# The first iteration's products in two passes, rounded parts before low parts, and VectorE's low parts in another order

## The chip, the cores and the metric

One core of one Trainium2 chip runs the whole kernel. Its engines are TensorE (PE: matmuls, with PEld for the weight loads), VectorE (DVE), ScalarE (ACT), GpSimd (POOL) and SyncE (SP, here only a queue that issues DMAs). Each works through its own queue in order; semaphores join them. The metric is the device time of one execution in microseconds, and the median of several is compared.

## The reference

The input x has 32 samples of 64 channels and 1024 points. Two levels follow each other, each `x = x + ffn(cond(x, style))`.

`cond` is four one-dimensional convolutions over the 64 channels whose weights depend on the sample (same, upsample with blur, same, downsample with blur). All four are linear with a bias, so the kernel folds the last three into one convolution per sample.

The ffn of level 0 is a routed adapter: `scores = x @ Wr.T` over 64 experts, the top 16 are kept and go through a softmax to gates, then `h = x @ A` (64 experts of rank 16, 1024 columns), `h` times the gate of its expert, and `out = 2 * (h @ B)`. The ffn of level 1 is a matmul with a 4-bit weight, dequantized with a scale and a zero for each column, and a bias.

## The kernel before, in words

**Precision.** TensorE multiplies in a rounded 32-bit format. So each operand is split into a rounded part `hi` (an ACTIVATE copy by ScalarE) and a low part `lo = whole - hi` (a subtraction by VectorE, helper `low`, L161), and each product is three matmuls: hi*hi, hi*lo, lo*hi. A and B are split so too, once, in eight chunks k of 128 rows: `act_a`/`dve_a` make `a_hi`, `a_lo`, `act_b`/`dve_b` make `b_hi`, `b_lo` (L952 and L161). `a_lo` lies over the loaded `a_raw`, `b_lo` over `b_raw`.

**Tiling.** Work goes by pairs of samples, 128 rows (two samples of 64 channels, or 128 tokens after the transposes). For level 0 a software pipeline over 16 pairs does in one pass the ffn of pair i and the convolutions of pair c = i+1. TensorE's order in one pass is: first layer of c, sample 0 (L175 to L177, 6 matmuls); transposes of the conv result of i (L739); first layer of c, sample 1; fold 3 of c (L593); hidden product, group 0 of i (`pe_hidden`, L766 to L768, 24 matmuls); fold 2 of c (L628); hidden groups 1 and 2; conv product of c, sample 0; transposes of the gated tile of i (L775); conv product of c, sample 1; adapter-out product of i, halves 0 and 1 (`pe_adapter_out`, L784 to L786, 24 matmuls each). Hidden group 0 (384 columns) holds the scores and the first 320 hidden columns, group 1 has 384, group 2 has 320. Each group has a PSUM bank of its own (`hidden_ps`).

**VectorE in one pass**: `dve_fold_start` (v_lo), `dve_turn` (low part of the transposed conv result, `xt`), `dve_layer1` (h_lo) for sample 0, `dve_fold3` (r_lo), `dve_layer1` for sample 1, `dve_route` (scores, top 16, exp, normalization), `dve_gate` 0, `dve_fold2` (e_lo and two copies), `dve_gate` 1 and 2, `dve_gated_turn` (low part of the turned gated tile, again `xt`), `split` (x_lo of the pair after next), `dve_first_residual`. ScalarE makes the rounded parts in the same order, with `act_exp` inside the routing.

**The first pass** (`first_pair(0, True)`) stands ahead of the loop over the others and has the splitting of A and B in it. Before it, ScalarE has made `a_hi` 0 to 6 and VectorE starts on `a_lo` 0 to 3. Inside it VectorE does `dve_a(4, 8)` right after `dve_turn`, `dve_b(0, 4)` after `dve_fold2`, and `dve_b(4, 8)` ahead of `dve_gated_turn`. ScalarE does `act_b(0, 3)` ahead of `act_exp` and `act_b(3, 8)` behind `act_fold2`. In hidden group 0 and adapter-out half 0 TensorE waits for the chunk's `a_lo` or `b_lo` ahead of each three matmuls. The queues' orders are written out by hand; no planner takes part.

Of the kernel before, what the change touches and what calls it, by code (L numbers as in the profile page):

```python
# [26 lines left out]
GROUPS = ((0, 384), (384, 768), (768, NE + KR))  # L27
ONES, QCOLS = 2, 342
KT = D // P
# [11 lines left out]
def program(nc, t):  # L41
    with ExitStack() as outer:
# [575 lines left out]
        def pe_fold2(pe, c, bufs, first=False):  # L618
            pe.wait_ge(S.fold3_ready, 2 * c + 2)
            if first:  # L620
                pe.wait_ge(S.lo["f2"], bufs.first_sample // B + 1)
            if not first or bufs.first_sample:
                pe.wait_ge(S.fold2_hi, 2 * c)
                pe.wait_ge(S.fold2_ready, c)
            for n, (tile, m, block) in enumerate(FOLD2):
                out = fold_ps[1][:, block * P:(block + 2) * P]
                for i, (w, r) in enumerate(((fold2_hi, bufs.r_hi), (fold2_hi, bufs.r_lo), (fold2_lo, bufs.r_hi))):
                    last = nc.tensor.matmul(out, windows(w)(tile), r[:, m:R_PAIRS:2, :, :], start=(n == 0 and i == 0),  # L628
                                            stop=(n == len(FOLD2) - 1 and i == 2), skip_group_check=True)
            last.then_inc(S.fold2_done, 1)  # L630
# [123 lines left out]

        hidden_ps = (prod_ps[0], prod_ps[1], turn_ps[1])

        def pe_hidden(pe, f, n, bufs, first=False):
            if n == 0:
                pe.wait_ge(S.xt_ready, 2 * f + 2)
                pe.wait_ge(S.x1_ready, 2 * f + 1)  # L760
            cols = slice(*GROUPS[n])
            out = hidden_ps[n][:, 0:cols.stop - cols.start]
            for k in range(KT):
                if first and n == 0:
                    pe.wait_ge(S.a_lo_ready, k + 1)
                nc.tensor.matmul(out, bufs.xt_hi[:, k, :], bufs.a_hi[:, k, cols], start=(k == 0), stop=False)  # L766
                nc.tensor.matmul(out, bufs.xt_hi[:, k, :], bufs.a_lo[:, k, cols], start=False, stop=False)  # L767
                last = nc.tensor.matmul(out, bufs.xt_lo[:, k, :], bufs.a_hi[:, k, cols], start=False, stop=(k == KT - 1))  # L768
            last.then_inc(S.hidden_done, 1)
# [8 lines left out]
        def pe_adapter_out(pe, f, bufs, n, first=False):  # L778
            pe.wait_ge(S.hgt_ready, 2 * f + 2)
            cols = slice(n * 512, (n + 1) * 512)  # L780
            for k in range(KT):
                if first and n == 0:
# [341 lines left out]
        def _(pe):  # L1124
# [16 lines left out]
            def first_step(i, first, conv=buf0):  # L1141
                c = i + 1
                second = conv is not buf0
                pe_layer1(pe, c, 0, conv, second)
                pe_turn(pe, i, buf0, False)
                pe_layer1(pe, c, 1, conv)
                pe_fold3(pe, c, conv, second)
                pe_hidden(pe, i, 0, buf0, first)
                pe_fold2(pe, c, conv, second)

            def first_products(i, first=False, conv=buf0):
                c = i + 1
# [3 lines left out]

            def first_pair(i, first):
                first_step(i, first)
                for n in (1, 2):
                    pe_hidden(pe, i, n, buf0)  # L1160
                first_products(i)
                for n in range(2):
                    pe_adapter_out(pe, i, buf0, n, first)

            first_pair(0, True)
            with pe.Fori(1, NPAIR - 2) as i:
# [94 lines left out]
        def _(act):  # L1261
# [44 lines left out]
            def first_step(i, first, conv=buf0):  # L1306
                c = i + 1
                second = conv is not buf0
                act_turn(act, i, buf0)
                if first:  # L1310
                    act_a(act, 7, KT)
                act_layer1(act, c, 0, conv)
                act_fold3(act, c, conv, second)
                act_layer1(act, c, 1, conv)
                if first:
                    act_b(act, 0, 3)
                act_exp(act, i, buf0)
                act_fold2(act, c, conv)
                if first:
                    act_b(act, 3, KT)  # L1320

            def first_pair(i, first=False):
                c = i + 1
# [107 lines left out]
        def _(v):  # L1431
# [34 lines left out]
            def first_step(i, first=False, conv=buf0):  # L1466

                c = i + 1
                dve_turn(v, i, buf0)
                if first:  # L1470
                    dve_a(v, 4, KT)
                dve_layer1(v, c, 0, conv)
                dve_fold3(v, c, conv)
                dve_layer1(v, c, 1, conv)

            def first_gates(i, first=False, conv=buf0):
                dve_route(v, i, buf0)
                dve_gate(v, i, 0, buf0)
                dve_fold2(v, i + 1, conv)
                if first:  # L1480
                    dve_b(v, 0, 4)

            def first_pair(i, first=False):
                c = i + 1
                dve_fold_start(v, c, buf0)
                first_step(i, first)
                first_gates(i, first)
                for n in (1, 2):
                    dve_gate(v, i, n, buf0)
                if first:  # L1490
                    dve_b(v, 4, KT)
                dve_gated_turn(v, i, buf0)
                split(c + 1, buf0)
                dve_first_residual(v, i, buf0)

# [166 lines left out]
```

## Time and profile before

| what | value |
|---|---|
| median of 3 runs | 946.69 us (945.65 to 946.77) |
| profiled execution: its own time | 946.65 us |
| its span (first to last instruction) | 945.0 us |
| TensorE busy (PE) | 920.9 us, 97% |
| weight loads (PEld) | 828.1 us, 88% |
| VectorE busy | 503.8 us, 53% |
| ScalarE busy | 410.0 us, 43% |
| GpSimd busy | 108.8 us, 12% |
| mean granted clock of TensorE | 0.987 |
| the chain that ended last: by engine | PE 89%, DVE 5%, ACT 2%, issue 2%, POOL 1% |

The busy shares are averages over the whole span. The matmul times of single rows include the drain of the pipeline, so that two rows overlap; the pitch of a stream is read from the starts. A wait is given for the instruction that stood still, with the one that released it.

### The profile page before, as it was taken

The page shows a single profiled execution, that of the slowest core. Times are in us where ns is not written, and L with a number is a line of the kernel's source. Part 1 is how long each engine was busy: PE and PEld are TensorE (multiplying, and loading weights), DVE is VectorE, ACT ScalarE, POOL GpSimd, SP SyncE. Part 2 cuts the span into 40 slices and gives each one's busy share as a digit, 9 for nine tenths or more (in the row PEclk, how much of TensorE's full clock was granted, in tenths as well). Part 3 has the DMA queues.
Part 4 walks back from the last instruction along what each step waited for, and adds up shares of the span by engine and source line. Part 5 has one row for each costly group of instructions (what it writes and reads, how often), then busy time and mean ns, then how long its engine had stood idle before and what let it go on. Part 6 is the DMA issues. An engine that isn't in the chain of part 4 may idle for free.

```text
span 945.0 us, 14656 instructions
## 1 busy us (share of the span) xinstructions
PE 920.9 (97%) x5020; PEld 828.1 (88%) x5020; DVE 503.8 (53%) x1079; ACT 410.0 (43%) x764; POOL 108.8 (12%) x137
## 2 busy tenths in 40 slices
PE   4889999999999999999999999999999999999998
PEld 4777998998998998998998998988999889998898
DVE  7795443443442442442452455578566656666555
ACT  2674333333333333432432433487455556555540
POOL 6100000000000000000000012130221112111121
PEclk9699999999999999999999999999999999999999
DMA  8701111011021011021021020225122222122111
GB/s 285 263 1 45 31 58 46 24 64 44 22 67 44 22 67 44 22 67 44 22 67 34 33 79 24 81 48 179 45 89 72 85 89 89 67 67 89 67 67 68
DMA packets 33004, 64.29 MB, mean 68 GB/s; under 512 B 11728, under 2 KB 13776, under 8 KB 32976
## 3 DMA queue, kind: packets, MB, share of 16 engines
q1 hardware_dynamic: 23904, 30.90, 11.0%
q0 software_dynamic: 9072, 33.03, 9.6%
q8 instruction: 16, 0.26, 0.1%
q14 instruction: 12, 0.10, 0.0%
HBM read 47.14 MB, written 16.78 MB: 68 GB/s over the span
## 4 chain that ended last, share of the span: by engine, by line
PE 89%; DVE 5%; ACT 2%; issue 2%; POOL 1%; SPq 0%; DMA 0%; ACTq 0%; DVEq 0%
PE conv_ps L175 9%; PE conv_ps L177 9%; PE conv_ps L176 9%; PE prod_ps L784 6%; PE prod_ps L786 6%; PE prod_ps L785 6%; PE fold_ps L628 5%; PE prod_ps L766 4%; PE prod_ps L768 4%; PE prod_ps L767 4%; PE prod_ps L860 4%; PE prod_ps L859 4%; PE fold_ps L593 3%; PE turn_ps L739 3%; PE turn_ps L768 2%; PE turn_ps L767 2%
## 5 line engine op out<-in xcount | busy, mean ns | idle before, releaser
L161 DVE TENSOR_TENSOR h_lo<-conv_ps,h_hi 64x512 fp32r<-64x512 f32 x128 | 88.3, 690 | 46.0 <-ACT h_hi L692 44.8
L175 PE MATMUL conv_ps<-h_hi,e_hi 128*128 128x512 f32 x256 | 104.3, 407 | 2.3 <-issue 1.8
L176 PE MATMUL conv_ps<-h_lo,e_hi 128*128 128x512 f32 x256 | 102.6, 401 | 0.0
L177 PE MATMUL conv_ps<-h_hi,e_lo 128*128 128x512 f32 x256 | 102.4, 400 | 0.0
L784 PE MATMUL prod_ps<-b_hi,xt 128*128 128x512 f32 x256 | 99.8, 390 | 1.5 <-DVE xt L161 1.5
L785 PE MATMUL prod_ps<-b_lo,xt 128*128 128x512 f32 x256 | 99.7, 389 | 0.0
L786 PE MATMUL prod_ps<-b_hi,xt 128*128 128x512 f32 x256 | 99.6, 389 | 0.0
L712 ACT ACTIVATE cond<-conv_ps,bias,demod_tab 128x510 f32<-128x510 f32 x64 | 49.8, 778 | 106.9 <-PE conv_ps L177 102.7
L766 PE MATMUL prod_ps<-a_hi,xt 128*128 128x384 f32 x256 | 86.9, 339 | 0.6 <-DVE a_lo L161 0.6
L768 PE MATMUL prod_ps<-a_hi,xt 128*128 128x384 f32 x256 | 86.5, 338 | 0.0
L767 PE MATMUL prod_ps<-a_lo,xt 128*128 128x384 f32 x256 | 86.4, 338 | 0.0
L859 PE MATMUL prod_ps<-quant,xt_hi 128*128 128x342 f32 x256 | 80.6, 319 | 0.0
L860 PE MATMUL prod_ps<-quant,xt_lo 128*128 128x342 f32 x256 | 80.5, 320 | 0.0
L745 ACT ACTIVATE xt<-turn_ps 128x512 fp32r<-128x512 f32 x32 | 17.4, 594 | 144.8 <-PE turn_ps L739 144.8
L844 DVE SCALAR_TENSOR_TENSOR res<-prod_ps,norm,res 128x512 f32<-128x512 f32 x32 | 23.9, 751 | 101.8 <-PE prod_ps L786 101.8
L796 ACT ACTIVATE xt<-turn_ps 128x512 fp32r<-128x512 f32 x32 | 17.4, 596 | 139.1 <-PE turn_ps L775 139.1
L161 DVE TENSOR_TENSOR xt<-turn_ps,xt 128x512 fp32r<-128x512 f32 x64 | 41.2, 685 | 65.8 <-ACT xt L796 48.9
L672 DVE SCALAR_TENSOR_TENSOR x_lo<-x_in,style_tab,x_hi 128x513 fp32r<-128x513 f32 x64 | 46.0, 760 | 55.5 <-ACT x_hi L663 55.4
L1067 POOL DMA_DIRECT2D x_after_first<-res x15 | 8.1, 542 | 479.8 <-DVE res L844 479.8
L175 PEld LDWEIGHTS conv_ps<-h_hi,e_hi 128*128 128x128 f32 x256 | 49.2, 192 | 12.9 <-issue 2.2
L177 PEld LDWEIGHTS conv_ps<-h_hi,e_lo 128*128 128x128 f32 x256 | 49.1, 192 | 11.5
L784 PEld LDWEIGHTS prod_ps<-b_hi,xt 128*128 128x128 f32 x256 | 48.0, 188 | 11.9 <-DVE xt L161 1.9
(245 smaller groups left out, 2197.7 us busy)
## 6 DMA issues: line engine op xcount, KB each, us to landing
x_in<-in_x SPq DMA_DIRECT2D x64, 128.0 KB, 2.8
res<-in_x POOLq DMA_DIRECT2D x16, 512.0 KB, 3.6
x_after_first<-res POOLq DMA_DIRECT2D x16, 512.0 KB, 2.9
x_in<-x_after_first SPq DMA_DIRECT2D x64, 128.0 KB, 2.7
res<-x_after_first POOLq DMA_DIRECT2D x16, 512.0 KB, 3.6
out_x<-res POOLq DMA_DIRECT2D x15, 512.0 KB, 2.9
a_raw<-in_adapter_in SPq DMA_DIRECT2D x8, 544.0 KB, 9.4
b_raw<-in_adapter_out SPq DMA_DIRECT2D x8, 512.0 KB, 6.5
```

What stands on the lines that cost most here:

```text
L161: return nc.vector.tensor_tensor(out, whole, hi.bitcast(F32), ALU.subtract)
L175: nc.tensor.matmul(out, hi(w), moving_hi(i), start=(i == 0), stop=False)
L176: nc.tensor.matmul(out, hi(w), moving_lo(i), start=False, stop=False)
L177: last = nc.tensor.matmul(out, lo(w), moving_hi(i), start=False, stop=(i == n - 1))
L766: nc.tensor.matmul(out, bufs.xt_hi[:, k, :], bufs.a_hi[:, k, cols], start=(k == 0), stop=False)
L767: nc.tensor.matmul(out, bufs.xt_hi[:, k, :], bufs.a_lo[:, k, cols], start=False, stop=False)
L768: last = nc.tensor.matmul(out, bufs.xt_lo[:, k, :], bufs.a_hi[:, k, cols], start=False, stop=(k == KT - 1))
L784: nc.tensor.matmul(prod_ps[n][:, :], bufs.xt_hi[:, k, :], bufs.b_hi[:, k, cols], start=(k == 0), stop=False)
L785: nc.tensor.matmul(prod_ps[n][:, :], bufs.xt_hi[:, k, :], bufs.b_lo[:, k, cols], start=False, stop=False)
L786: last = nc.tensor.matmul(prod_ps[n][:, :], bufs.xt_lo[:, k, :], bufs.b_hi[:, k, cols], start=False, stop=(k == KT - 1))
L859: nc.tensor.matmul(out, bufs.xt_hi[:, k, :], bufs.quant[:, k, cols], start=(k == 0), stop=False)
L860: last = nc.tensor.matmul(out, bufs.xt_lo[:, k, :], bufs.quant[:, k, cols], start=False, stop=(k == KT - 1))
```

## The change

Only the first pass of level 0 changes. On TensorE the products with the rounded parts `a_hi` (by xt_hi and xt_lo) of all three hidden groups come first, and those with `a_lo` (by xt_hi) of all three groups after them; likewise `b_hi` for both halves of adapter-out, and then `b_lo`. Fold 2 moves from behind hidden group 0 to behind the rounded products of groups 0 and 1. Waits per chunk are now on `a_hi`, `a_lo`, `b_hi` and `b_lo`, ahead of two, one, two and one matmuls. On ScalarE `act_fold2` comes ahead of `act_exp`, and `act_b(3, 8)` behind both. On VectorE `dve_a(4, 8)` moves behind both `dve_layer1` and `dve_fold3`, `dve_fold2` ahead of the routing, and of the `b_lo` chunks one comes between the gates and `dve_gated_turn`, the other seven behind it.

```diff
+        def pe_hidden_hi(pe, f, n, bufs):
             if n == 0:
                 pe.wait_ge(S.xt_ready, 2 * f + 2)
                 pe.wait_ge(S.x1_ready, 2 * f + 1)
             cols = slice(*GROUPS[n])
             out = hidden_ps[n][:, 0:cols.stop - cols.start]
             for k in range(KT):
-                if first and n == 0:
+                if n == 0:
+                    pe.wait_ge(S.a_hi_ready, k + 1)
+                for w in (bufs.xt_hi, bufs.xt_lo):
+                    nc.tensor.matmul(out, w[:, k, :], bufs.a_hi[:, k, cols], start=(k == 0 and w is bufs.xt_hi), stop=False)
+
+        def pe_hidden_lo(pe, f, n, bufs):
+            cols = slice(*GROUPS[n])
+            out = hidden_ps[n][:, 0:cols.stop - cols.start]
+            for k in range(KT):
+                if n == 0:
                     pe.wait_ge(S.a_lo_ready, k + 1)
+                last = nc.tensor.matmul(out, bufs.xt_hi[:, k, :], bufs.a_lo[:, k, cols], start=False, stop=(k == KT - 1))
+            last.then_inc(S.hidden_done, 1)
...
+        def pe_adapter_out_hi(pe, f, bufs, n):
             pe.wait_ge(S.hgt_ready, 2 * f + 2)
...
+                if n == 0:
+                    pe.wait_ge(S.b_hi_ready, k + 1)
+                for w in (bufs.xt_hi, bufs.xt_lo):
+                    nc.tensor.matmul(prod_ps[n][:, :], w[:, k, :], bufs.b_hi[:, k, cols], start=(k == 0 and w is bufs.xt_hi), stop=False)
...
+        def pe_adapter_out_lo(pe, f, bufs, n):
...
+                if n == 0:
                     pe.wait_ge(S.b_lo_ready, k + 1)
+                last = nc.tensor.matmul(prod_ps[n][:, :], bufs.xt_hi[:, k, :], bufs.b_lo[:, k, cols], start=False, stop=(k == KT - 1))
+            last.then_inc(S.out_done, 1)
...
-                pe_hidden(pe, i, 0, buf0, first)
-                pe_fold2(pe, c, conv, second)
+                if first:
+                    for n in range(3):
+                        pe_hidden_hi(pe, i, n, buf0)
+                        if n == 1:
+                            pe_fold2(pe, c, conv)
+                    for n in range(3):
+                        pe_hidden_lo(pe, i, n, buf0)
...
-                for n in range(2):
-                    pe_adapter_out(pe, i, buf0, n, first)
+                if first:
+                    for n in range(2):
+                        pe_adapter_out_hi(pe, i, buf0, n)
+                    for n in range(2):
+                        pe_adapter_out_lo(pe, i, buf0, n)
...
                 if first:
                     act_b(act, 0, 3)
-                act_exp(act, i, buf0)
-                act_fold2(act, c, conv)
-                if first:
+                    act_fold2(act, c, conv)
+                    act_exp(act, i, buf0)
                     act_b(act, 3, KT)
...
                 dve_turn(v, i, buf0)
-                if first:
-                    dve_a(v, 4, KT)
                 dve_layer1(v, c, 0, conv)
                 dve_fold3(v, c, conv)
                 dve_layer1(v, c, 1, conv)
+                if first:
+                    dve_a(v, 4, KT)
 
             def first_gates(i, first=False, conv=buf0):
+                if first:
+                    dve_fold2(v, i + 1, conv)
                 dve_route(v, i, buf0)
                 dve_gate(v, i, 0, buf0)
-                dve_fold2(v, i + 1, conv)
-                if first:
-                    dve_b(v, 0, 4)
+                if not first:
+                    dve_fold2(v, i + 1, conv)
...
                 if first:
-                    dve_b(v, 4, KT)
+                    dve_b(v, 0, 1)
                 dve_gated_turn(v, i, buf0)
+                if first:
+                    dve_b(v, 1, KT)
```

## Rows read from the trace of the kernel before

**Rows 1.** Windows: length, busy us (instructions) per engine, granted clock, DMA share.
```profile
46.04:87.29 41.25, 37.37 (x195) 31.80 (x193) 30.42 (x49) 24.65 (x39) 0.00 (x0) 1.00 0.05 13
87.29:123.11 35.82, 35.82 (x195) 32.25 (x193) 14.92 (x35) 12.32 (x24) 1.07 (x2) 1.00 0.15 45
...
158.80:600.00 441.20, 441.20 (x2392) 397.50 (x2391) 193.95 (x458) 157.84 (x305) 20.83 (x39) 1.00 0.14 46
```

**Rows 2.** Waits, 46.04 to 87.29: total, times, longest.
```profile
PE prod_ps L784 <- DVE xt L161: 1.5, 1, 1.5
...
PE fold_ps L628 <- DVE r_lo L612: 1.4, 1, 1.4
...
PE prod_ps L766 <- DVE a_lo L161: 0.6, 2, 0.4
```

**Rows 3.** Timeline of TensorE, first pass: start us, duration us, what.
```profile
51.56 0.45 PE L766 MATMUL prod_ps<-a_hi,xt 128*128 128x384 f32 x1
...
54.31 0.34 PE L766 MATMUL prod_ps<-a_hi,xt 128*128 128x384 f32 x1
...
68.14 0.39 PE L175 MATMUL conv_ps<-h_hi,e_hi 128*128 128x512 f32 x1
...
71.70 0.48 PE L175 MATMUL conv_ps<-h_hi,e_hi 128*128 128x512 f32 x1
...
76.23 0.50 PE L784 MATMUL prod_ps<-b_hi,xt 128*128 128x512 f32 x1 [1.50 <-DVE xt L161]
```

**Rows 4.** Timeline of TensorE, second pass.
```profile
92.04 0.34 PE L766 MATMUL prod_ps<-a_hi,xt 128*128 128x384 f32 x1
...
94.68 0.34 PE L766 MATMUL prod_ps<-a_hi,xt 128*128 128x384 f32 x1
...
105.77 0.40 PE L175 MATMUL conv_ps<-h_hi,e_hi 128*128 128x512 f32 x1
```

**Rows 5.** Timeline of VectorE, first pass.
```profile
51.42 4.88 DVE L161 TENSOR_TENSOR a_lo<-a_raw,a_hi 128x1088 fp32r<-128x1088 f32 x4
56.23 1.39 DVE L161 TENSOR_TENSOR h_lo<-conv_ps,h_hi 64x512 fp32r<-64x512 f32 x2
...
59.85 0.23 DVE L812 COPY scores<-prod_ps 128x64 f32<-128x64 f32 x1
...
63.01 0.48 DVE L830 TENSOR_TENSOR cond<-prod_ps,gate 128x320 f32<-128x320 f32 x1
63.41 0.68 DVE L161 TENSOR_TENSOR e_lo<-fold_ps,e_hi 128x512 fp32r<-128x512 f32 x1
...
64.95 4.63 DVE L161 TENSOR_TENSOR b_lo<-b_raw,b_hi 128x1024 fp32r<-128x1024 f32 x4
69.50 0.55 DVE L830 TENSOR_TENSOR cond<-prod_ps,gate 128x384 f32<-128x384 f32 x1
...
70.36 4.62 DVE L161 TENSOR_TENSOR b_lo<-b_raw,b_hi 128x1024 fp32r<-128x1024 f32 x4
74.90 1.28 DVE L161 TENSOR_TENSOR xt<-turn_ps,xt 128x512 fp32r<-128x512 f32 x2
76.45 1.42 DVE L672 SCALAR_TENSOR_TENSOR x_lo<-x_in,style_tab,x_hi 128x513 fp32r<-128x513 f32 x2 [0.27 <-ACT x_hi L663]
```

**Rows 6.** Timeline of ScalarE, first pass.
```profile
52.95 0.59 ACT L692 ACTIVATE h_hi<-conv_ps 64x512 fp32r<-64x512 f32 x1
...
55.69 0.59 ACT L692 ACTIVATE h_hi<-conv_ps 64x512 fp32r<-64x512 f32 x1
...
60.70 0.35 ACT L791 ACTIVATE gate_exp<-scores,neg_max 128x64 f32<-128x64 f32 x1 [1.45 <-DVE neg_max L814]
...
62.90 4.86 ACT L952 ACTIVATE b_hi<-b_raw 128x1024 fp32r<-128x1024 f32 x5
71.55 1.09 ACT L796 ACTIVATE xt<-turn_ps 128x512 fp32r<-128x512 f32 x2 [3.79 <-PE turn_ps L775]
```

**Rows 7.** Groups by line and shape, 46.04 to 87.29: busy us, mean ns.
```profile
L766 PEld LDWEIGHTS prod_ps<-a_hi,xt 128*128 128x128 f32 x16 | 3.0, 188 | 1.6 <-DVE a_lo L161 1.2 <-DVE xt L161 0.4
```

More of the change, by code:

```diff
@@ L755, in program @@
         hidden_ps = (prod_ps[0], prod_ps[1], turn_ps[1])
-        def pe_hidden(pe, f, n, bufs, first=False):
+        def pe_hidden_hi(pe, f, n, bufs):
             if n == 0:
@@ L763, in pe_hidden @@
             for k in range(KT):
-                if first and n == 0:
-                    pe.wait_ge(S.a_lo_ready, k + 1)
+                if n == 0:
[7 more added lines that the diff above has]
+                if n == 0:
+                    pe.wait_ge(S.a_lo_ready, k + 1)
+                last = nc.tensor.matmul(out, bufs.xt_hi[:, k, :], bufs.a_lo[:, k, cols], start=False, stop=(k == KT - 1))
+            last.then_inc(S.hidden_done, 1)
+        def pe_hidden(pe, f, n, bufs):
+            if n == 0:
+                pe.wait_ge(S.xt_ready, 2 * f + 2)
+                pe.wait_ge(S.x1_ready, 2 * f + 1)
+            cols = slice(*GROUPS[n])
+            out = hidden_ps[n][:, 0:cols.stop - cols.start]
+            for k in range(KT):
                 nc.tensor.matmul(out, bufs.xt_hi[:, k, :], bufs.a_hi[:, k, cols], start=(k == 0), stop=False)
@@ L776, in pe_gated_turn @@
                 last.then_inc(S.gated_turned, 1)
-        def pe_adapter_out(pe, f, bufs, n, first=False):
+        def pe_adapter_out_hi(pe, f, bufs, n):
             pe.wait_ge(S.hgt_ready, 2 * f + 2)
@@ L781, in pe_adapter_out @@
             for k in range(KT):
-                if first and n == 0:
-                    pe.wait_ge(S.b_lo_ready, k + 1)
+                if n == 0:
[3 more added lines that the diff above has]
+        def pe_adapter_out_lo(pe, f, bufs, n):
+            cols = slice(n * 512, (n + 1) * 512)
+            for k in range(KT):
+                if n == 0:
+                    pe.wait_ge(S.b_lo_ready, k + 1)
+                last = nc.tensor.matmul(prod_ps[n][:, :], bufs.xt_hi[:, k, :], bufs.b_lo[:, k, cols], start=False, stop=(k == KT - 1))
+            last.then_inc(S.out_done, 1)
+        def pe_adapter_out(pe, f, bufs, n):
+            pe.wait_ge(S.hgt_ready, 2 * f + 2)
+            cols = slice(n * 512, (n + 1) * 512)
+            for k in range(KT):
                 nc.tensor.matmul(prod_ps[n][:, :], bufs.xt_hi[:, k, :], bufs.b_hi[:, k, cols], start=(k == 0), stop=False)
@@ L1147, in first_step @@
                 pe_fold3(pe, c, conv, second)
-                pe_hidden(pe, i, 0, buf0, first)
-                pe_fold2(pe, c, conv, second)
+                if first:
[5 more added lines that the diff above has]
+                        pe_hidden_lo(pe, i, n, buf0)
+                else:
+                    pe_hidden(pe, i, 0, buf0)
+                    pe_fold2(pe, c, conv, second)
             def first_products(i, first=False, conv=buf0):
@@ L1158, in first_pair @@
                 first_step(i, first)
-                for n in (1, 2):
-                    pe_hidden(pe, i, n, buf0)
+                if not first:
+                    for n in (1, 2):
+                        pe_hidden(pe, i, n, buf0)
                 first_products(i)
-                for n in range(2):
-                    pe_adapter_out(pe, i, buf0, n, first)
+                if first:
[3 more added lines that the diff above has]
+                        pe_adapter_out_lo(pe, i, buf0, n)
+                else:
+                    for n in range(2):
+                        pe_adapter_out(pe, i, buf0, n)
             first_pair(0, True)
@@ L1316, in first_step @@
                     act_b(act, 0, 3)
-                act_exp(act, i, buf0)
-                act_fold2(act, c, conv)
-                if first:
+                    act_fold2(act, c, conv)
+                    act_exp(act, i, buf0)
                     act_b(act, 3, KT)
+                else:
+                    act_exp(act, i, buf0)
+                    act_fold2(act, c, conv)
             def first_pair(i, first=False):
@@ L1474, in first_step @@
                 dve_layer1(v, c, 1, conv)
+                if first:
+                    dve_a(v, 4, KT)
             def first_gates(i, first=False, conv=buf0):
+                if first:
+                    dve_fold2(v, i + 1, conv)
                 dve_route(v, i, buf0)
                 dve_gate(v, i, 0, buf0)
-                dve_fold2(v, i + 1, conv)
-                if first:
-                    dve_b(v, 0, 4)
+                if not first:
+                    dve_fold2(v, i + 1, conv)
             def first_pair(i, first=False):
```

## The prediction

> **What bounds the kernel now.** I read the windows first, cut at the places where TensorE begins the first convolution layer of a new pair. The first pass through the level-0 loop body (the one that the change touches) lasts 41.25 us, the next 35.82 us [rows 1]. Both issue the same TensorE work. In the second pass TensorE is busy 35.82 of 35.82 us, and in the long stretch from 158.80 to 600.00 it is busy 441.20 of 441.20 us: there only TensorE's own stream sets the end. In the first pass it is busy 37.37 of 41.25 us, so 3.88 us are waits, and the excess over a normal pass is 41.25 - 35.82 = 5.43 us. Its granted clock is 1.00 in all three stretches, the 2.4 GHz level, so the clock is not a part of the difference.
>
> The waits of that stretch name what is late [rows 2]: the adapter-out product for the gated low part 1.5 us, fold 2 for `r_lo` 1.4 us, the hidden product for `a_lo` 0.6 us. All three are released by VectorE; the rest of the 3.88 us is small and lies mostly ahead of the hidden products. In the order of time VectorE's queue shows why [rows 5]: four `a_lo` subtractions from 51.42 stand in front of the conv low parts, which start at 56.23, and four `b_lo` subtractions from 70.36 stand in front of the gated low part at 74.90. TensorE stands still for work that is ready but queued behind work that is not urgent.
>
> **The change part by part.** Nothing is added or removed on VectorE, ScalarE and TensorE but waits: the same 72 hidden, 15 fold-2 and 48 adapter-out matmuls, the same eight `a_lo` and eight `b_lo`. So the sum is a new schedule of three queues, from 51.56 on, where the first hidden matmul starts [rows 3]. Up to there nothing moves: `v_lo` and the low part of xt wait for ScalarE as before, which makes this part of the pass 0.77 us longer than in the next one (51.56 - 46.04 = 5.52 against 92.04 - 87.29 = 4.75 [rows 1, 3, 4]). The ceiling of the gain is therefore 5.43 - 0.77 = 4.66 us.
>
> TensorE, hidden products and fold 2. Undisturbed they take 105.77 - 92.04 = 13.73 us [rows 4]; now they take 68.14 - 51.56 = 16.58 us [rows 3]. After a wait the first matmul costs some 0.1 us more: 15 matmuls took 54.31 - 51.56 = 2.75 us in the first pass, 94.68 - 92.04 = 2.64 us in the second. If nothing holds it, TensorE comes to the conv product at 51.56 + 13.73 + 0.11 = 65.40, a gain of 2.74 us. The conditions:
> - fold 2 (now behind two high groups of 16 matmuls at 2.64 / 15 = 0.176 us) starts at 51.67 + 5.63 = 57.3. `r_lo` needs `r_hi`, and no longer stands behind `a_lo`: VectorE makes the first conv low part when ScalarE's first `h_hi` ends at 52.95 + 0.59 = 53.54 [rows 6], for 1.39 us, then `r_lo` (0.84 us, what the two conv low parts leave of 59.85 - 56.23 [rows 5]), to 55.8. Met by 1.5 us, so the fold-2 wait goes.
> - the second conv low part starts when `h_hi` ends at 55.69 + 0.59 = 56.28 [rows 6], and takes to 57.67. The four late `a_lo` cost 56.23 - 51.42 = 4.81 us [rows 5] and end at 62.5. The low hidden products are the last 8 x (0.176 + 0.176 + 0.147) = 4.0 us of the block (0.147 by 320/384 of 0.176), so they start at 61.4 and ask for the eighth `a_lo` at 62.6. Met by 0.1 us: every 0.1 us that VectorE is late here costs 0.1 us, down to nothing.
>
> VectorE after it. `e_lo` and its copies 64.95 - 63.41 = 1.54 us, to 64.0; the routing 63.01 - 59.85 = 3.16 us, to 67.2; first gate 0.40 us, the other two 70.36 - 69.50 = 0.86 us, to 68.4 [rows 5]. `e_lo` at 64.0 is ready for the conv product at 65.40. TensorE wants the gated tile after one conv product, which takes with the eight transposes 71.70 - 68.14 = 3.56 us: twelve matmuls of 512 columns at 0.23 us (11.06 / 48, below) are 2.77 us of it and the transposes 0.8 us, so it wants the first half at 65.40 + 2.77 = 68.2 and the other at 68.6. Both are met by 0.1 to 0.2 us.
>
> ScalarE is where I expect the one wait that is left. Its exp stands behind the routing's maximum, 60.70 - 59.85 = 0.85 us after its start, now 64.85, and ends at 65.2; the five late `b_hi` (4.86 us, [rows 6]) are behind it and end at 70.1. Only then does it copy the gated tiles, 1.09 us for two: 70.6 and 71.2. VectorE follows with both low parts in 1.28 us, 70.65 to 71.93. It has put one `b_lo` (4.55 / 4 = 1.14 us, from 64.95 to 69.50) into the gap before, 68.4 to 69.6, and is free. TensorE is through the second conv product at 65.40 + 3.56 + 2.87 = 71.83 (twelve matmuls as in the 2.77 us of the first, with 0.1 us of refill), and starts adapter-out at 71.98. Now it starts at 76.23. The block takes 87.29 - 76.23 = 11.06 us and would end at 83.04.
>
> `b_lo`. Seven more from 71.93, 8.0 us, to 79.9. The low adapter products begin after 32 high ones, 32 x 0.228 = 7.3 us (11.06 / 48 with the refill off), at 79.3, and ask for the eighth `b_lo` at 80.9: met by 1.0 us. Then both `x_lo` (1.42 us, to 81.3) for the next pass, whose first matmul is at 83.04 and wants the first of them at 80.7: met by 2.3 us. The load of the pair after that is issued once `x_lo` is there, some 3.5 us later than now, and is not read before ScalarE's split in the next pass, some 30 us on. The residual follows the last matmul as it does now. From 83.04 on everything is the present schedule moved up.
>
> The sum: 87.29 - 83.04 = 4.25 us, of it 2.74 us in the hidden block and 1.5 us before adapter-out. If the last wait were nil too it would be 4.5 us, the ceiling 4.66 us. Against the profiled execution (946.65 us; span 945.0 us and 1.65 us around it) that makes 942.4 us; that execution lies 0.04 us under the median of the three runs, so the same number holds for a median.
>
> **A rule weighed.** The change puts 32 waits into the stream, one before every two matmuls (high) or one (low), where 16 stand now, one before every three. A wait could hold up the weight load behind it. The rows say no for one per three: the eight waits on `a_lo` cost nothing but the refill (2.75 against 2.64 us [rows 3, 4]), although a weight load takes 188 ns [rows 7]. With one matmul between waits no row exists. I take zero, the value of the nearest row; the other end is a load and a refill at each, 32 x (0.188 + 0.11) = 9.5 us. The Trainium skill (TensorE: Matmul & The Clock Gate, Back-to-back issue gap) has the spacing set by load and matmul together, in a window that pulls loads ahead. Its section on LDWEIGHTS puts a load of 128 columns at 107 ns; by that the other end would be 32 x (0.107 + 0.11) = 6.9 us and the time 949.3 us. The trace's 188 ns differs from it and decides.
>
> **The rivals.**
> 1. VectorE's queue, not TensorE, paces the block. From 56.28 to 71.93 the chain of low parts, routing, gates, ScalarE's `b_hi` and the gated low part has margins of 0.1 to 0.2 us against TensorE. For it: the margins. Against it: every duration is from the same instructions in the same stretch. If the chain of 15.65 us comes 10% longer, 1.6 us are lost: 944.0 us.
> 2. The waits in the low groups alone (one matmul each) expose their weight loads, without a refill: 16 x 0.188 = 3.0 us, so 945.4 us, within the bound of no change. The same bound would hold a gain given back later; against that stand 441.20 busy of 441.20 us.
> 3. Slower: all 32 waits cost a load and a refill, in the hidden and adapter-out groups of the first pass. 9.5 us lost against 4.25 us gained: 951.9 us. The kernel is slower than before from 15 such waits on (15 x 0.298 = 4.5), and by over 1.9 us from 21. Against it: the eight waits of rows 3 and 4.
>
> **How the numbers follow.** About 0.2% (1.9 us) is what a measurement of this kernel tells from no change. The forecast has 0.80, rival 1 has 0.10 (0.02 of it with a loss over 2.35 us, which ends inside the bound), rival 2 has 0.06, rival 3 has 0.04. Faster: 0.80 + 0.08 = 0.88; same: 0.02 + 0.06 = 0.08; slower: 0.04. The range goes from the ceiling (942.0) less 0.8 us for the spread of runs (945.65 to 946.77) up past rival 1: 941.2 to 944.6 us.
>
> **What would show it.** In the changed profile the pass takes near 37.0 us instead of 41.25; the waits on `r_lo` and `a_lo` vanish or stay under 0.2 us; the wait of adapter-out falls from 1.5 us to 0.3 us or less and is released by the gated low part behind ScalarE's copy; the first hidden matmul still starts 5.5 us into the pass; there is no wait on `b_lo`; the next pass stays at 35.8 us. I am wrong if matmuls between two waits are spaced wider than 0.176 and 0.228 us, if TensorE waits for `a_lo` or for a gate for more than 0.5 us, or if any later pass grows.

## The result and the profile after

The changed kernel takes 940.72 us (median of 6 runs, 940.13 to 941.92), the kernel before 945.98 us (6 runs, 945.48 to 946.77): ratio 0.9945, 95% interval 0.9932 to 0.9958. It is faster by 5.3 us where 4.2 was forecast, and 940.72 lies below the range of 941.2 to 944.6. A second set, on one chip, has 941.53 against 946.30 us, ratio 0.9947 (0.9933 to 0.9961).

The windows of the changed kernel are cut where those of before are [rows 1]: head, first pass, second pass, rest. Columns: length, then busy us (instructions) of TensorE, its weight loads, VectorE, ScalarE, GpSimd, then the granted clock and DMA (share and GB/s). The window of the second pass is 0.05 us too long (the third pass begins at 118.30), so that pass takes 35.72 us, against 35.82 before.

```profile
0.00:45.59 45.59, 30.32 (x120) 26.22 (x121) 35.46 (x102) 21.46 (x35) 18.32 (x33) 0.78 0.84 284
45.59:82.58 36.99, 36.62 (x195) 31.80 (x193) 30.69 (x49) 24.40 (x39) 0.00 (x0) 1.00 0.01 2
82.58:118.35 35.77, 35.77 (x195) 32.21 (x194) 14.91 (x35) 12.32 (x24) 1.07 (x2) 1.00 0.17 58
118.35:940.20 821.85, 817.43 (x4516) 737.78 (x4514) 422.83 (x894) 351.56 (x667) 88.89 (x102) 1.00 0.18 60
```

The first pass took 41.25 us and takes 36.99 us: 4.26 us less, with 4.25 forecast. What lies behind it is the same: 945.0 - 87.29 = 857.71 us before, 940.2 - 82.58 = 857.62 us now. The head is 0.45 us shorter, in code that is the same.

The waits of the first pass, answering to [rows 2]. The three waits of TensorE's matmuls named in [rows 2] are gone; the one on `v_lo` stays. The weight loads (PEld), which run ahead of the matmuls, still wait for two tiles that the change is about:

```profile
PE fold_ps L593 <- DVE v_lo L579: 0.3, 1, 0.3
...
PEld prod_ps L775 <- DVE a_lo L161: 0.3, 1, 0.3
PEld prod_ps L804 <- DVE xt L161: 0.2, 1, 0.2
```

The eighth `a_lo` in VectorE's timeline:

```profile
60.90 1.28 DVE L161 TENSOR_TENSOR a_lo<-a_raw,a_hi 128x1088 fp32r<-128x1088 f32 x1
```

It ends at 62.18 us, and the wait for it holds the matmuls up: the low products of group 0 start at 61.93, 62.23 and 62.51 around it, where the others are 0.175 us apart, so it costs 0.23 us. The other profiles of the changed kernel have this wait too (0.2 us in each).

TensorE's timeline, answering to [rows 3] (start, duration, what). The products of one kind now stand together and, but for that wait, follow each other without a gap:

```profile
51.10 5.88 PE L767 MATMUL prod_ps<-a_hi,xt 128*128 128x384 f32 x32
...
58.53 2.50 PE L767 MATMUL turn_ps<-a_hi,xt 128*128 128x320 f32 x16
60.87 3.20 PE L775 MATMUL prod_ps<-a_lo,xt 128*128 128x384 f32 x16
63.91 1.34 PE L775 MATMUL turn_ps<-a_lo,xt 128*128 128x320 f32 x8
65.08 0.39 PE L175 MATMUL conv_ps<-h_hi,e_hi 128*128 128x512 f32 x1
...
71.63 7.49 PE L804 MATMUL prod_ps<-b_hi,xt 128*128 128x512 f32 x32
78.95 3.79 PE L811 MATMUL prod_ps<-b_lo,xt 128*128 128x512 f32 x16
```

VectorE's timeline, answering to [rows 5]; against times of before, 0.45 us go to the shorter head:

```profile
57.28 4.89 DVE L161 TENSOR_TENSOR a_lo<-a_raw,a_hi 128x1088 fp32r<-128x1088 f32 x4
62.21 0.69 DVE L161 TENSOR_TENSOR e_lo<-fold_ps,e_hi 128x512 fp32r<-128x512 f32 x1
...
63.75 0.23 DVE L846 COPY scores<-prod_ps 128x64 f32<-128x64 f32 x1
...
68.17 1.21 DVE L161 TENSOR_TENSOR b_lo<-b_raw,b_hi 128x1024 fp32r<-128x1024 f32 x1
70.20 1.29 DVE L161 TENSOR_TENSOR xt<-turn_ps,xt 128x512 fp32r<-128x512 f32 x2 [0.82 <-ACT xt L830]
71.41 8.03 DVE L161 TENSOR_TENSOR b_lo<-b_raw,b_hi 128x1024 fp32r<-128x1024 f32 x7
79.36 1.41 DVE L672 SCALAR_TENSOR_TENSOR x_lo<-x_in,style_tab,x_hi 128x513 fp32r<-128x513 f32 x2
```

The gated low part ends at 71.49 and adapter-out starts at 71.63, directly behind the conv product.

### The profile page after: what moved, and what is told of

The parts are those of the page before. It is cut to its first block, busy times and chain, and to the rows that moved or that the text cites. A ratio compares the mean times of both kernels' runs of the same rounds, so it can differ in the third digit from the quotient of the medians.

```text
span 940.2 us, 14656 instructions
## 1 busy us (share of the span) xinstructions
PE 920.1 (98%) x5020; PEld 828.0 (88%) x5020; DVE 503.9 (54%) x1079; ACT 409.7 (44%) x764; POOL 108.3 (12%) x137
## 4 chain that ended last, share of the span: by engine, by line
PE 91%; DVE 3%; ACT 2%; issue 1%; POOL 1%; SPq 0%; DMA 0%; ACTq 0%; DVEq 0%
PE conv_ps L175 9%; PE conv_ps L177 9%; PE conv_ps L176 9%; PE fold_ps L628 6%; PE prod_ps L818 5%; PE prod_ps L820 5%; PE prod_ps L819 5%; PE prod_ps L785 5%; PE prod_ps L787 4%; PE prod_ps L786 4%; PE prod_ps L894 4%; PE prod_ps L893 4%; PE fold_ps L593 3%; PE turn_ps L739 3%; PE turn_ps L787 2%; PE turn_ps L786 2%
## 5 line engine op out<-in xcount | busy, mean ns | idle before, releaser
L818 PE MATMUL prod_ps<-b_hi,xt 128*128 128x512 f32 x240 | 93.5, 390 | 0.0
L819 PE MATMUL prod_ps<-b_lo,xt 128*128 128x512 f32 x240 | 93.4, 389 | 0.0
L820 PE MATMUL prod_ps<-b_hi,xt 128*128 128x512 f32 x240 | 93.4, 389 | 0.0
L785 PE MATMUL prod_ps<-a_hi,xt 128*128 128x384 f32 x240 | 81.1, 338 | 0.0
L787 PE MATMUL prod_ps<-a_hi,xt 128*128 128x384 f32 x240 | 81.1, 338 | 0.0
L786 PE MATMUL prod_ps<-a_lo,xt 128*128 128x384 f32 x240 | 81.0, 338 | 0.0
L176 PEld LDWEIGHTS conv_ps<-h_lo,e_hi 128*128 128x128 f32 x256 | 49.1, 192 | 9.4
```

What stands on the lines that cost most here:

```text
L176: nc.tensor.matmul(out, hi(w), moving_lo(i), start=False, stop=False)
```

## The experiments

### Is the gain in the first pass alone? (after_again, before_look1 to 3, after_look2 and 3)

These are the two kernels unchanged, for more times (after_again) and more profiles (all six).

> The changed kernel once more, for its time against the kernel before on one chip. In its profile the first pass took 36.99 us (before: 41.25), which is 4.26 us, and the stretch behind it 857.62 us (before: 857.71); but the six timed runs stand 5.26 us apart (945.98 and 940.72). Theory A: only the 4.26 us are the change's, and the rest is the spread of the head of the program (the first 46 us, with DMA arrivals and the half clock), which differs from execution to execution; then a new set gives a gain that may lie anywhere from 3.5 to 5.3 us, and the profile again has a pass of 37.0 us, while the head differs by some tenths from 45.59 us. Theory B: the change also shortens the head or the rest by about 1 us in every run; then the gain is 5.2 us again and the head of its profile is about 1 us shorter than 46.04 us each time.

> The kernel before, unchanged, for one more profile. In the profiles so far TensorE's granted clock falls to the half level in some executions and not in others: around 657 to 667 us in before, after and hidden_half, not in after_again, adapter_half and early_fold; and right behind the waits of the first pass in adapter_half (58.3 to 61.6 us) and hidden_half (69.9 to 76.7 us), but not in the profile of before, whose waits there are the same as in adapter_half. Theory C: the waits of the first pass bring such a fall in a part of the executions of the kernel before; the changed kernel has no wait there and so no fall, and this is what it gains beyond 4.26 us. Then this profile has, with a chance of perhaps a half, a stretch at the half clock between 55 and 62 us or between 75 and 80 us, and where it has one the pass is 42.5 to 43 us and not 41.25. Theory A: the clock in the first pass is as in the first profile of before each time, and the pass is 41.2 to 41.3 us.

> The kernel before once more, for its profile, cut in three: head (to the first matmul of the first pass), first pass, rest. So far head 46.04 and 45.98, pass 41.25 and 41.25, rest 857.71 and 857.27 us. In every profile in which the granted clock falls to half around 657 to 667 us the rest is 857.3 to 857.8 us, in those without it 855.9 to 856.1 us. Theory D: the kernel before has this fall in most executions (2 of 2 so far) and the changed kernel in fewer (1 of 2), because the low-work stage near 655 us comes at another moment of the clock's own rhythm; that is what the medians stand apart beyond 4.3 us. Then this profile has the fall and a rest near 857.5 us. Theory A (chance alone): the fall comes in both kernels alike, in about half of the executions.

> The changed kernel once more, for its profile. So far head 45.59 and 46.75, pass 36.99 and 36.95, rest 857.62 (with the fall of the clock near 660 us) and 855.9 us (without). Theory D: no fall, rest near 856.0 us, clock 0.991. Theory A: with or without it alike. Both: a pass of 37.0 us.

> As before_look2, for the count. Theory D: the fall near 660 us, rest near 857.5 us; theory A: in one of two.

> As after_look2, for the count. Theory D: no fall near 660 us, rest near 856.0 us; theory A: in one of two.

The spans, cut in three; "fall" says whether the clock falls to half near 660 us.

| profile | head | first pass | rest | fall |
|---|---|---|---|---|
| before | 46.04 | 41.25 | 857.71 | yes |
| before_look1 | 45.98 | 41.25 | 857.27 | yes |
| before_look2 | 45.05 | 41.21 | 857.54 | yes |
| before_look3 | 46.22 | 41.20 | 857.98 | yes |
| after | 45.59 | 36.99 | 857.62 | yes |
| after_again | 46.75 | 36.95 | 855.90 | no |
| after_look2 | 45.74 | 37.01 | 857.85 | yes |
| after_look3 | 45.27 | 36.98 | 857.65 | yes |

The pass repeats within 0.06 us. The head, the same code in all, goes from 45.05 to 46.75 us. The rest differs by 1.7 us with the fall. Its place in after, and the stretch of the same work in after_again, where the small matmuls ahead of it start 1.04 us later (655.78 against 654.74); columns as above:

```profile
657.00:661.50 4.50, 4.50 (x15) 3.44 (x15) 1.72 (x4) 0.68 (x6) 3.89 (x2) 0.62 0.00 0
```

```profile
658.04:662.54 4.50, 4.50 (x24) 3.83 (x24) 2.22 (x5) 1.87 (x9) 3.88 (x2) 1.00 0.00 0
```

TensorE is busy all the time in both, but with most of the stretch at the half clock it issues 15 matmuls where it issues 24 at the full one. Theory D's first prediction, no fall in after_look2 and after_look3, failed twice. The means of the four are 45.82, 41.23 and 857.63 us before and 45.84, 36.98 and 857.26 us after: 4.6 us apart, 4.25 of it in the pass and 0.37 in the rest, most of it by the one execution without the fall.

The milder half of theory D, that the fall comes less often in the changed kernel, has support in the clocks of the timed runs. A fall of 3.4 us at the half clock takes 3.4 / 2 / 940 = 0.0018 off the mean granted clock of an execution. All four profiles with a mean clock of 0.991 (after_again, after_late, early_fold, early_fold2) have no fall behind the head. Of the 11 timed runs of the changed kernel four have 0.991, six 0.989 and one 0.987. Of the 47 timed runs of before in the later sets none has 0.991, 15 have 0.989, 31 have 0.987 and one 0.986. The means, 0.9895 and 0.9876, lie about one fall apart. How much time that is the clocks do not tell: the half clock also fills more or less of the head (mean 0.78 there in before and after, 0.82 in after_again), and before can have a fall inside its first pass that costs nothing, as before_look3 shows.

before_look3 has a second fall, the one that theory C asked for, right behind the wait on `r_lo`. Its windows and all the waits of TensorE in its pass:

```profile
46.22:58.20 11.98, 10.18 (x51) 7.97 (x49) 11.16 (x15) 11.81 (x19) 0.00 (x0) 1.00 0.00 1
58.20:62.00 3.80, 3.29 (x15) 3.29 (x16) 3.24 (x13) 1.55 (x3) 0.00 (x0) 0.55 0.00 0
62.00:87.42 25.42, 25.42 (x131) 22.07 (x129) 15.98 (x24) 11.25 (x18) 0.00 (x0) 1.00 0.07 21
```

```profile
PE fold_ps L628 <- DVE r_lo L612: 1.4, 1, 1.4
...
PE prod_ps L766 <- DVE a_lo L161: 0.6, 2, 0.4
...
PE fold_ps L593 <- DVE v_lo L579: 0.3, 1, 0.3
```

Yet its pass is 41.20 us. The wait on the gated low part, 1.5 us in [rows 2], is missing among the matmuls' waits: TensorE came there later by what the fall took, while VectorE, which sets that moment, was not slowed. So theory C has the fall right and its cost wrong (42.5 to 43 us were expected): it came in one of four profiles of before, and there a later wait absorbed it.

### Do the waits of before cost more than their length? (before_filled)

```diff
+        def filler(ps, n):
+            for _ in range(n):
+                nc.tensor.matmul(ps[:, :], w1_hi[:, 0, :], buf0.a_hi[:, 0, 0:512], start=True, stop=True)
...
                 if first and n == 0:
+                    filler(turn_ps[0], {6: 2, 7: 3}.get(k, 0))
                     pe.wait_ge(S.a_lo_ready, k + 1)
...
                 pe_hidden(pe, i, 0, buf0, first)
+                if first:
+                    filler(turn_ps[0], 5)
                 pe_fold2(pe, c, conv, second)
...
                 first_products(i)
+                if first:
+                    filler(prod_ps[0], 6)
```

> The kernel before with its waits of the first pass filled: 16 extra matmuls of 512 columns into banks that nobody reads (2 and 3 ahead of the chunks 6 and 7 of hidden group 0, 5 ahead of fold 2, 6 ahead of adapter-out). They do nothing for the result and end before what TensorE waits for. Theory C (waits bring falls of the clock): never a half-clock stretch in the first pass, and a median 0.5 to 1.0 us below before though the pass is no shorter than 41.2 us. Theory A (waits cost their length alone): the same median as before within 0.3 us, or slightly above.

946.47 us against 946.47 (ratio 1.0001, 0.9992 to 1.0010). Its pass:

```profile
45.61:86.81 41.20, 40.53 (x210) 34.78 (x209) 30.42 (x49) 24.66 (x39) 0.00 (x0) 1.00 0.04 14
```

TensorE is busy 40.53 of 41.20 us instead of 37.37 of 41.25 [rows 1], and nothing is gained. That speaks against theory C as an account of the missing 1 us (the median was to fall by 0.5 to 1.0 us), and shows that the releases by VectorE's queue set the pass, not the amount of TensorE's work. The mean clock of its runs (0.991 in one, 0.989 in seven, 0.987 in three of 11) is a little above that of before, with no gain in time.

### The halves and the single queues (adapter_half, hidden_half, tensor_only, queues_only)

adapter_half undoes the hidden block: `pe_hidden` with three matmuls per chunk, fold 2 behind group 0, `dve_a(4, 8)` behind `dve_turn`, `dve_fold2` behind the first gate, `act_exp` ahead of `act_fold2`. hidden_half undoes the other half:

```diff
-                if first:
-                    for n in range(2):
-                        pe_adapter_out_hi(pe, i, buf0, n)
-                    for n in range(2):
-                        pe_adapter_out_lo(pe, i, buf0, n)
...
+                for n in range(2):
+                    pe_adapter_out(pe, i, buf0, n, first)
...
+                if first:
+                    dve_b(v, 0, 4)
...
-                    dve_b(v, 0, 1)
+                    dve_b(v, 4, KT)
                 dve_gated_turn(v, i, buf0)
-                if first:
-                    dve_b(v, 1, KT)
```

tensor_only keeps all edits of TensorE and undoes those of VectorE and ScalarE; queues_only does the reverse.

> Hidden products, fold 2, a_lo and the routing in the old order; only adapter-out in two passes and b_lo one ahead of the gated low part and seven behind it. Theory A (queues alone): VectorE is free for the gated low part when ScalarE has the tiles, about 73.4 us by the times of before, so the 1.5 us wait goes and the pass is 41.25 - 1.66 = 39.6 us; the waits on r_lo and a_lo stay; 2.6 us of the gain belong to the hidden half. Theory B (the waits on each chunk cost weight loads): the adapter block is longer than 11.1 us.

> The other half: hidden products in two passes, a_lo and e_lo moved, adapter-out and b_lo in the old order (four b_lo behind the first gate, four ahead of the gated low part). Theory A: the routing now ends 4 us later than before, and eight b_lo (9.1 us) stand between it and the gated low part: gates 1 and 2 come at 72.3 us instead of 68.4, the transposes wait 4.5 us, adapter-out starts near 78.5 us by the times of before, and the pass is 44.0 us, 2.8 us longer than before; the time is about 2.7 us above before. Rival: the halves add up and the hidden half is worth its own 2.7 us: a pass of 38.6 us.

> TensorE's order of the changed kernel with the queues of VectorE and ScalarE as before. The schedule of the queues: r_lo still behind four a_lo, so fold 2 waits 1.3 us; the routing starts only when all three rounded groups, fold 2 and the low products of group 0 are through (64.2 us by the times of before, against 59.85) and e_lo behind the routing comes at 69.3 us, so the conv product waits 2.5 us; eight b_lo then stand ahead of the gated low part, adapter-out starts near 80.7 us and the pass is 45.7 us, 4.5 us longer than before. Rival: the order of the matmuls alone brings a good part of the gain (a pass of 37 to 40 us).

> VectorE and ScalarE in the new order with TensorE's order as before. The schedule of the queues: hidden group 0 asks for the fifth a_lo at 53.8 us by the times of before, and gets it at 58.9, the eighth at 62.5; fold 2 comes behind it at 63.1, and the routing behind e_lo at 67.2 us; adapter-out starts near 79.1 us and then waits for each b_lo of half 0 to 87 us: a pass of 46.8 us, 5.5 us longer than before. Rival: the VectorE order alone brings a good part of the gain, since it is VectorE that all three waits name (a pass of 37 to 40 us).

| kernel | pass expected | pass measured | time, and before on the same chip |
|---|---|---|---|
| adapter_half | 39.6 | 40.91 | 944.11, 946.30 (0.9973, 0.9961 to 0.9986) |
| hidden_half | 44.0 | 44.03 | 948.23, 946.30 (1.0017, 1.0007 to 1.0026) |
| tensor_only | 45.7 | 45.74 | 951.44 (one execution), 946.47 |
| queues_only | 46.8 | 47.56 | 951.52 (one execution), 946.20 |

The rivals fell: the halves do not add up, and neither TensorE's order nor VectorE's and ScalarE's brings a gain alone. Theory B of adapter_half fell too: its adapter-out block takes 87.03 - 76.16 = 10.87 us, so the waits on each chunk cost nothing. By their passes tensor_only is 4.5 us and queues_only 6.3 us slower than before, by their single executions 5.0 and 5.3 us; all queues together are over 4 us faster. In tensor_only TensorE's matmuls stand still for 6.8 us in all, 2.6 of it ahead of the conv product, where 2.5 were expected. In hidden_half VectorE's order shows the reason: the gates 1 and 2 stand behind four `b_lo`, and TensorE waits for them.

```profile
66.30 0.48 DVE L866 TENSOR_TENSOR cond<-prod_ps,gate 128x320 f32<-128x320 f32 x1
66.70 4.62 DVE L161 TENSOR_TENSOR b_lo<-b_raw,b_hi 128x1024 fp32r<-128x1024 f32 x4
71.24 0.55 DVE L866 TENSOR_TENSOR cond<-prod_ps,gate 128x384 f32<-128x384 f32 x1
71.71 0.48 DVE L866 TENSOR_TENSOR cond<-turn_ps,gate 128x320 f32<-128x320 f32 x1
72.11 4.62 DVE L161 TENSOR_TENSOR b_lo<-b_raw,b_hi 128x1024 fp32r<-128x1024 f32 x4
76.64 1.28 DVE L161 TENSOR_TENSOR xt<-turn_ps,xt 128x512 fp32r<-128x512 f32 x2
```

```profile
71.85 1.97 PE L794 MATMUL turn_ps<-ident,cond 128*128 128x128 f32 x8 [4.41 <-DVE cond L866]
```

The granted clock is at its half level here from about 70 to 77 us, and the pass is as expected even so: the gated low part, which adapter-out needs, is ready only at 77.92.

In queues_only it is TensorE that asks too early; its waits (total, times, longest):

```profile
PE prod_ps L787 <- DVE a_lo L161: 5.1, 1, 5.1
PE prod_ps L822 <- DVE b_lo L161: 0.7, 4, 0.2
```

The granted clock is 0.93 in the mean over its pass, half from 59.5 to 66 us, behind the long wait; the 0.8 us over the expected pass are put down to that, without a test of their own.

adapter_half missed its number by 1.3 us, with no wait more than expected. The windows of its pass show a fall of the clock:

```profile
46.12:58.20 12.08, 10.18 (x51) 7.96 (x49) 11.25 (x15) 11.91 (x19) 0.00 (x0) 1.00 0.00 1
58.20:61.60 3.40, 2.95 (x14) 2.95 (x15) 2.94 (x12) 1.49 (x3) 0.00 (x0) 0.54 0.00 0
61.60:87.03 25.43, 25.43 (x131) 22.46 (x131) 16.31 (x25) 11.24 (x18) 0.00 (x0) 0.99 0.03 10
```

This is the fall of before_look3 at the same place, behind the same waits, but here no later wait absorbs it. Its runs go from 942.63 to 945.38 us, and the lowest is the only one with a mean clock of 0.991, thus without any fall behind the head; the other five have 0.989. That fits 39.6 us as the pass without the fall, but no profile of such a run was taken.

### How much room has VectorE? (three_ahead)

```diff
-                    dve_b(v, 0, 1)
+                    dve_b(v, 0, 3)
                 dve_gated_turn(v, i, buf0)
...
-                    dve_b(v, 1, KT)
+                    dve_b(v, 3, KT)
```

> The changed kernel with three b_lo ahead of the gated low part in place of one: 2 x 1.14 us more on VectorE before the subtraction that adapter-out waits for. In the changed kernel that subtraction ran from 70.20 to 71.49 us and adapter-out began at 71.63 without a wait. By the schedule of the queues it now begins at 71.6 and ends at 72.9: a wait of 1.3 us, a pass of 38.3 us. Rival: VectorE has room there and the pass stays at 37.0 us. Theory C adds that such a wait brings the half clock in some executions, for 1.3 to 1.7 us more.

The pass is 38.32 us (38.3 expected), and the wait is there:

```profile
73.92 6.41 PE L804 MATMUL prod_ps<-b_hi,xt 128*128 128x512 f32 x27 [1.12 <-DVE xt L161]
```

944.01 us against 946.47 (0.9972, 0.9958 to 0.9985). So VectorE has under 1 us of room there in the changed kernel (2.28 us more of it cost 1.3), as the prediction's margins said. The time is 2.5 us above after_again's 941.53, where the pass accounts for 1.3; its one profile has no fall in the pass (clock 1.00), and its timed runs have mean clocks of 0.989 (three) and 0.987 (two). Whether falls in the pass, as theory C has it, or the spread of the runs make up the rest stays open.

### The fall near 660 us (before_late, after_late)

```diff
+                    if L == 1:
+                        for _ in range(6):
+                            nc.tensor.matmul(prod_ps[0][:, 0:384], w1_hi[:, 0, :], fold2_hi[:, :], start=True, stop=True)
                     last = products(prod_ps[1][:, side * B:(side + 1) * B], (2 + side, 1 + side, side), windows(s.down_hi), windows(s.down_lo), one(s.edge_hi), one(s.edge_lo))
```

> The kernel before with 12 extra matmuls of 384 columns (six ahead of each side) in the stage of 18 small matmuls (32 columns) near 660 us, behind which the granted clock has fallen to half in all four profiles of before. They write a bank that nobody reads and cost 12 x 0.176 = 2.1 us. If the small matmuls bring the fall (1.7 us), it is gone and the time is 0.4 us above before; if not, 2.1 us above.

> The same 12 extra matmuls in the changed kernel. Theory D (a part of the gain is that this fall comes less often in the changed kernel): with the fall gone from both, before_late and after_late stand only 4.25 us apart, the first pass alone, and after_late is 1 us or more above the changed kernel. Theory A (sampling of the runs): they stand apart as before and after do, by 4.3 to 5.2 us, and the fall says nothing on it. In both profiles: rest of the program 855.9 + 2.1 = 858.0 us.

Neither profile has the fall; the windows of before_late and after_late there:

```profile
660.00:670.00 10.00, 10.00 (x60) 8.98 (x59) 3.80 (x8) 3.83 (x13) 4.74 (x2) 1.00 0.00 1
```

```profile
655.00:665.00 10.00, 9.74 (x59) 8.61 (x58) 4.66 (x10) 4.90 (x14) 4.42 (x2) 1.00 0.00 1
```

The rests are 858.09 and 858.25 us, as expected (858.0), the passes 41.21 and 37.00 us. The times are 947.25 us (1.0009 of before, 1.0000 to 1.0018) and 942.65 us (0.9958, 0.9945 to 0.9972). before_late is 1.05 us above before, where 0.4 was expected if the fall is in every execution of before and goes, and 2.1 if it is in none; the interval (0 to 1.7 us) leaves out only the second. The clocks say the same: 0.990 or 0.991 in four of the 11 runs of before_late and in none of the 15 of before beside them, with means of 0.9890 and 0.9874, nearly one fall apart. Three runs of before_late still have 0.987, so whether the extra matmuls take the fall away every time is not shown. The two times stand 4.6 us apart, between the 4.25 of theory D and the 5.3 and 4.8 of the unchanged pairs, with some 1 us of noise: by its times the pair does not settle between theories A and D.

### A version that beats both (early_fold, early_fold2)

```diff
             act_a(act, 1, 5)
+            act_fold_start(act, 1, buf0)
+            nc.scalar.preload_act_table(ACT.Exp)
             ready(0)
...
-            nc.scalar.preload_act_table(ACT.Exp)
...
             split(1, buf0)
+            dve_fold_start(v, 1, buf0)
             edge_vector(v, 0, set0, 4)
...
-                act_fold_start(act, c, buf0)
+                if not first:
+                    act_fold_start(act, c, buf0)
...
-                dve_fold_start(v, c, buf0)
+                if not first:
+                    dve_fold_start(v, c, buf0)
```

> The changed kernel, and on top of it ScalarE loads the Exp table and makes v_hi of pair 1, and VectorE v_lo, in the gap in which both wait for the edge values (ScalarE 39.4 to 43.5 us, VectorE 38.9 to 42.9 us in the changed kernel). Theory A: the wait of fold 3 for v_lo and the late conv tile are all that is left of the excess of the first pass: TensorE reaches the hidden products 4.75 us into the pass instead of 5.52, the pass is 36.2 us, and the time is 0.8 us below the changed kernel. Rival: the table load delays the eviction of pair 0 instead, and nothing is gained.

> early_fold once more, since its first time (940.21 us, against 941.53 us of the changed kernel) rested on five runs. Its pass was 35.79 us against 36.95, so 1.2 us below the changed kernel is expected, and a pass of 35.8 us again.

940.21 us (0.9933, 0.9919 to 0.9946) and 939.46 us (0.9925, 0.9912 to 0.9939), the fastest here. The pass is 35.79 and 35.78 us, and TensorE has no wait in it:

```profile
45.85:81.63 35.78, 35.78 (x194) 32.23 (x193) 29.94 (x47) 22.46 (x36) 0.00 (x0) 1.00 0.02 5
```

ScalarE's timeline in early_fold2 shows the table load and `v_hi` in the gap, and the conv tile's copy at 47.89, released by the transposes:

```profile
37.80 0.79 ACT L574 ACTIVATE v_hi<-down_T,scale 128x192 fp32r<-128x192 f32 x2
38.60 1.28 ACT L1348 ACT_TABLE_LOAD   x1
43.77 0.78 ACT L712 ACTIVATE cond<-conv_ps,bias,demod_tab 128x510 f32<-128x510 f32 x1 [3.89 <-DVE cond_edge L533]
...
47.89 1.09 ACT L745 ACTIVATE xt<-turn_ps 128x512 fp32r<-128x512 f32 x2 [0.48 <-PE turn_ps L739]
```

Expected were 36.2 us: the 0.4 us of the last `a_lo` and of restarts behind waits went as well (the weight loads have no wait left either). early_fold stands 1.3 us below the changed kernel of the same set (941.53 us). The two moves, the table load and `v_hi` with `v_lo`, were not tried apart.

## Why the prediction was right in the mechanism and wrong in the number

- What bounds the pass: right. VectorE's order, not TensorE's work (before_filled).
- Fold 2, `r_lo`, `a_lo`: right but for one margin. The wait for `r_lo` is gone. The eighth `a_lo`, said to be "met by 0.1 us", came late, and its weight load waited 0.3 us. So the block ends 13.98 us after its start (65.08 - 51.10), with 13.84 forecast (65.40 - 51.56).
- VectorE's chain: right. From the fifth `a_lo` (57.28) to the gated low part (70.20) it took 12.92 us; forecast were 12.98 (57.67 to 70.65).
- The one wait that was to be left, 0.15 us before adapter-out: not there. The weight load stood 0.2 us for the tile (ready at 71.49), but the matmul began at 71.63, on the beat of the one before it (71.40).
- `b_lo` and `x_lo`: right, no wait on either.
- Waits between single matmuls that hold nothing up: zero, as taken. The 32 high adapter products go at (78.95 - 71.63) / 32 = 0.229 us, the 16 low ones at (82.58 - 78.95) / 16 = 0.227 us. That settles the rule weighed and the second and third rivals. The prediction's own ground for it was thinner than it says: the 15 matmuls of [rows 3] cover five of the eight waits on `a_lo`, and two of the other three held.
- The pass: 36.99 us, with 37.0 forecast. The agreement to 0.01 us is in part luck: the hidden block took 0.14 us more, the stretch from there to adapter-out 0.03 us less (71.63 - 65.08 = 6.55 against 6.58), and the adapter-out block 0.11 us less (10.95 against 11.06).
- What is behind the pass: moved up unchanged in the profiles that have the fall near 660 us (857.62 against 857.71 us), not in after_again, which has none (855.90 us).

The step that failed is the last term, "that makes 942.4 us", and with it the low end, "the ceiling (942.0) less 0.8 us for the spread of runs". It has two parts. First, it took one execution and three runs (946.65 and 946.69 us) for the kernel before, and set the gain of the pass against them. Six runs of before have 945.98 us, so 0.7 us of the miss of 1.7 us is the base. Second, it put every difference outside the pass at nothing ("from 83.04 on everything is the present schedule moved up"). The other 1.0 us (5.3 against 4.25) is not in the pass, and the changed code does not reach beyond it. The runs show two things outside the pass that differ from execution to execution: the head by up to 1.7 us, and the fall near 660 us by 1.7 us. The fall came in 4 of 4 profiles of before and 3 of 4 of after. The prediction read the clock in its three windows (1.00) and not at 661 to 666 us, where before had it. The clocks of the timed runs (0.991 in 4 of 11 of the changed kernel, in none of 47 of before) point to a fall that comes less often in the changed kernel. That this makes up the 1.0 us, rather than sampling, is not shown: the second set (4.8 us), the means of the profiles (4.6) and the pair with the extra matmuls (4.6) lie between 4.25 and 5.3, and the intervals reach about 1.2 us to each side. Both sets' intervals hold 4.25 us (0.9955). Why the fall should come less often behind an earlier pass stays open.

## What to carry to other kernels

When an operand must be prepared while the engine that uses it already runs, order the products by when their operands are ready, and give the preparing engine first what others wait for and last what only the tail of the products needs. Such a reordering is one edit over all the queues: TensorE's new order alone and that of VectorE and ScalarE alone were slower here. Cut by stage instead, the adapter-out half was 2.2 us faster alone and the hidden half 1.9 us slower alone. And a schedule read from one profile gave the difference of the changed stretch to 0.1 us here, while the total carries what varies between executions; forecast the gain from the stretch and the total from many runs.

## What the runs showed of the hardware that was not expected

TensorE's granted clock fell to its lower level (1.2 GHz) for some 3 to 4 us without a long wait ahead of it. It did so behind a stage of 18 matmuls of 32 columns with one wait of 0.22 us (near 660 us, in 11 of the 16 profiles in which that stage was unchanged, in neither of the two with 12 matmuls of 384 columns put in), and behind waits of 0.16, 0.40 and 1.4 us spread over 4 us (2 of 6 profiles that have those waits: adapter_half and before_look3). The same program has it in one execution and not in another. Near 660 us, where TensorE is the bound, it cost 1.7 us (a rest of 857.3 to 858.0 us with it, of 855.7 to 856.1 us without); in before_look3, where a wait on VectorE followed, it cost nothing.
